# A graph-network kernel whose weight pieces are loaded in transfers of unequal height: 64, 24, 36 and 4 partitions in every third piece

## What is computed

```python
h = relu(layernorm(x))
q, k, v = h @ wq.T + bq, h @ wk.T + bk, h @ wv.T + bv
q2, k2, v2 = q @ wiq.T + biq, k @ wik.T + bik, v @ wiv.T + biv    # 16 heads of 64
scores = einsum('hnd,hmd->hnm', q2, k2) / 8 + mask                # mask: -inf where no edge
x = x + (softmax(scores) @ v2) @ wo.T + bo

h = relu(layernorm(x))
u = h @ root + bias
for r in range(8):                                                # mean over edges of type r
    u = u + (segment_sum(h[src] * (type == r), dst) / max(count, 1)) @ weight[r]
z = concat(u, h) @ w_gate + b_gate
x = x + tanh(u) * z + h * (1 - z)
```

## Time and profile before

| | us |
|---|---|
| median of three runs | 228.53 |
| the three runs | 226.64, 228.53, 229.94 |
| the profiled execution | 227.98 |
| its span | 225.8 |
| PE busy | 216.0 (96%) |
| DVE busy | 80.6 (36%) |
| POOL busy | 23.2 (10%) |
| ACT busy | 22.3 (10%) |
| packets of queue q1, share of 16 engines | 88.5% |

### The profile page before, as it was taken

The page is one execution under the profiler, slowest core; times in us unless marked ns, Lnnn a source line. Parts: engine busy times, 40 slices in busy tenths (PEclk is TensorE's granted clock), DMA queues, the critical chain, the costliest instruction groups (busy, mean ns, idle before and its releaser), DMA issues.

```text
span 225.8 us, 10194 instructions
## 1 busy us (share of the span) xinstructions
PE 216.0 (96%) x4797; PEld 210.1 (93%) x4797; DVE 80.6 (36%) x138; ACT 22.3 (10%) x41; POOL 23.2 (10%) x53
## 2 busy tenths in 40 slices
PE   2999998998999999999999999999999999999994
PEld 2889988998999999898999999999999999999993
DVE  2479638050399930555738500000000000000624
ACT  2550000000020110132033000000000000000101
POOL 2271005500000000010000940000000000000000
PEclk9999999999999999999999999999999999999999
DMA  6999999999999999999999799999999999998002
GB/s 225 366 393 422 421 422 421 380 376 385 363 386 385 328 383 376 363 359 399 412 360 379 209 306 398 328 383 388 398 380 361 369 350 338 356 363 332 6 3 70
DMA packets 14684, 77.01 MB, mean 341 GB/s; under 512 B 4874, under 2 KB 5138, under 8 KB 5428
## 3 DMA queue, kind: packets, MB, share of 16 engines
q1 hardware_dynamic: 14112, 75.96, 88.5%
q10 hardware_dynamic: 532, 0.42, 0.6%
HBM read 75.97 MB, written 0.39 MB: 338 GB/s over the span
## 4 chain that ended last, share of the span: by engine, by line
PE 95%; DMA 2%; issue 1%; DVE 1%; ACT 0%
PE acc L780 81%; PE acc L1027 4%; DMA x_sb<-in_x 2%; PE turn L968 1%; PE side L828 1%; PE side L968 1%; PE side L1027 1%; PE turn L856 1%; DVE stats L505 1%; PE acc L798 1%; PE turn L798 0%; PE turn L872 0%; PE side L839 0%; PE turn L839 0%; PE acc L872 0%
## 5 line engine op out<-in xcount | busy, mean ns | idle before, releaser
L780 PE MATMUL acc<-mean,raw 128*64 128x96 f32 x2048 | 84.7, 246 | 0.0
L780 PEld LDWEIGHTS acc<-mean,raw 128*64 128x64 f32 x2048 | 84.6, 137 | 0.0
L780 PE MATMUL acc<-hT,raw 128*64 128x96 f32 x1024 | 44.4, 247 | 0.3 <-issue 0.3
L780 PEld LDWEIGHTS acc<-hT,raw 128*64 128x64 f32 x1024 | 42.9, 137 | 1.4 <-issue 1.1
L743 DVE TENSOR_TENSOR uT<-acc,uT 128x384 f32<-128x384 f32 x2 | 1.1, 558 | 80.9 <-PE acc L780 80.9
L780 PE MATMUL acc<-kT,raw 128*64 128x96 f32 x512 | 22.1, 246 | 0.8 <-issue 0.8
L780 PEld LDWEIGHTS acc<-kT,raw 128*64 128x64 f32 x512 | 21.5, 137 | 1.3 <-issue 1.2
L780 PE MATMUL acc<-qT,raw 128*64 128x96 f32 x512 | 22.0, 246 | 0.7 <-issue 0.7
L780 PEld LDWEIGHTS acc<-qT,raw 128*64 128x64 f32 x512 | 21.4, 137 | 1.0 <-issue 1.0
L780 PE MATMUL acc<-uT,raw 128*64 128x96 f32 x256 | 12.6, 266 | 0.0
L780 PEld LDWEIGHTS acc<-uT,raw 128*64 128x64 f32 x256 | 12.2, 152 | 0.3 <-ACT uT L409 0.2
(11 more groups left out here) (177 smaller groups left out, 148.3 us busy)
## 6 DMA issues: line engine op xcount, KB each, us to landing
raw<-in_weights SPq DMA_DIRECT2D x284, 256.0 KB, 4.7
raw<-in_weights SPq DMA_DIRECT2D x1, 1024.0 KB, 5.9
x_sb<-in_x SPq DMA_DIRECT2D x1, 192.0 KB, 3.5
x_sb<-in_x ACTq DMA_DIRECT2D x1, 192.0 KB, 3.7
out<-out_rows SPq DMA_DIRECT2D x1, 192.0 KB, 2.1
out<-out_rows ACTq DMA_DIRECT2D x1, 144.0 KB, 2.4
out<-out_rows SPq DMA_DIRECT2D x1, 48.0 KB, 2.2
bias_rows<-in_biases ACTq DMA_DIRECT2D x1, 36.0 KB
```

Source lines behind the costliest of these rows:

```text
L780: mm = pe.matmul(a[g * HD:(g + 1) * HD, b, c * N:(c + 1) * N], raw[:, s, at:at + HD], moving(k0 + k), start=opens and k0 == 0 and c == 0 a ...
```

## The change

`transfers(n)` gets a second case. Every piece whose number leaves 1 when divided by 3 (1, 4, 7, ..., 70: 24 of the 72) is loaded in four transfers of unequal height: 64 partitions (all the even ones), 24 (the odd ones from 1 to 47), 36 (the odd ones from 49 to 119) and 4 (121, 123, 125, 127). Piece 0 and the other 47 pieces are loaded as they were. The bytes, the number of transfers and the semaphore counts stay.

```diff
 def transfers(n):
 
+
     if n == 0:
         return [slice(0, P)]
+    if n % 3 == 1:
+        return [slice(0, P, 2), slice(1, 49, 2), slice(49, 121, 2), slice(121, P, 2)]
     return [slice(j, P, 4) for j in range(4)]
```

## The result

The changed kernel took 272.23 us in the median of four runs (270.79 to 277.4), the kernel before 228.39 us beside it (226.64 to 229.94). The ratio is 1.190, with a 95% interval of 1.177 to 1.203: 19% slower. The forecast was 232.2 us and a range that ended at 240. The profiled execution of after has 270.79 us, its span 268.6 us against 225.8, 42.8 us more.

A forecast was written before the change was run, and what follows sets the result against it. PE, busy 216.0 of 225.8 us, was taken to bound the kernel. Weights staying hidden added nothing and late instructions 3.7 us (5.5 against 1.8), so 228.5 + 3.7 = 232.2 us, range 226.5 to 240.

The forecast's parts named there:

- its three gaps: PE's waits ending in "issue" at 29.7, 35.8 and 52.7 us, 1.8 us together, read as late instruction packets.
- How many engines share a transfer: Weight stream: largest divisor of the rows up to 16, so 64, 24, 36, 4 go to 16, 12, 12, 4 engines.
- A row costs 0.311 us whatever its transfer: Weight stream: engine time per 8 KB row, read from 30 to 34 us before the change and taken as fixed.
- Load of an engine in three pieces: DMA engines: 24 rows, 7.46 us before; after, 26 rows on four (8.09 us), 25 on eight, 20 on four.
- the first result: Weight stream: at 2.70 to 2.87 us a piece the last piece lands before 218.6 us, so weights stay hidden at no cost.
- the price of the second: PE's instruction fetch: packets late behind a lasting queue on the heavier engines, 5.5 us against 1.8, so +3.7 us.
- SP's issue of the short transfers: SP's issues of 24, 36 and 4 rows: 0.27 to 0.6 us each, so 7.6 to 8.6 us per three pieces.
- The bound from ACT's 274 ns: SP's issues: lower limit for short transfers, from one on 6 engines that ACT issued in 0.274 us.
- The rival with this end: Weight stream: narrow transfers at half rate, 3.11 us a piece against 2.97 allowed, weights late, 238 us; chance 0.10.
- Instructions late by 3.7 us more: PE's instruction fetch: the main case, late packets costing 5.5 us against 1.8, total 232.2 us; chance 0.44.
- The price of 0.36 us per late border: PE's instruction fetch: 1.8 us of gaps over 5 packet borders, charged per border while the queue is long.
- The upper bound of 18 us: Late-instruction term: long queue on all twelve engines to the end and gaps twice as long, +18 us.

The follow-up runs named there:

- f3: Kernel before with every third piece in two transfers of 64 partitions, even and odd, in place of four: 239.7 us, ratio 1.052.
- g4: Kernel before, with SP waiting ahead of the third transfer of each piece until the piece two before has landed: 233.7 us, ratio 1.020.
- k3: f3 with SP waiting in the middle of each piece until the piece two before has landed: 235.6 us, ratio 1.023.
- f2: Changed kernel with every third piece split 64, 16, 32, 16 instead, all on 16 engines with 8 rows each: 280.1 us, ratio 1.229.
- f4: Kernel before with every third piece in four equal transfers of 32 contiguous partitions: 333.9 us in two runs.
- k1: Kernel before with all pieces but the first in four transfers of 32 contiguous partitions: 346.2 us, ratio 1.516.
- k2: Kernel before with every third piece in step-4 transfers of 32, 32, 32, 24 and 8 rows: 248.8 us; 248.3 us when run again.
- m1: Changed kernel with the unequal transfers in every sixth piece in place of every third: 247.6 us, ratio 1.085.
- f1: Changed kernel with the transfers of 24 and 36 rows joined, so every third piece is 64, 60, 4: 284.1 us, ratio 1.247.
- g3: Kernel before, with SP waiting before each piece until the piece two before has landed: 258.1 us, ratio 1.133.
- k4: Kernel before, with SP's wait in mid-piece for the piece two before, for pieces 2 to 20 only: 230.6 us, ratio 1.010.

## Why the prediction was wrong, point by point

**PE is the bound and its three gaps are late instructions: right.** The gaps of after stand multiples of 256 instructions apart, each ends behind a packet of q8, f3 makes them grow with the queue while its rows stay fast, and g4 and k3 make them shrink.

**How many engines share a transfer: right.** q1 has 13632 packets, as worked out.

**A row costs 0.311 us whatever its transfer: wrong, and this is the step that failed.** "Load of an engine in three pieces" counted rows (26 against 24 on the heaviest engines) and priced them at the rate of the uniform stream. Equal loads (f2) gave the same slow rows as after. The row went from 0.347 to 0.428 us by the measure of the table, 23% on the whole stream, where the count of rows had given 8% on four engines. 72 x 8 x 0.428 = 247 us of stream, so it can't stay within the 2.97 us a piece that the lead allowed (3.42 now). With it fell the first result, that the weights stay hidden, and the price of the second, the late instructions, was far too low.

**SP's issue of the short transfers lies between 0.27 and 0.6 us: wrong.** L308 from 1.3 us on in after, two issues a line (min, median, max), so that each line hands one value to the next; the order is 128, 64, 24, 36 and 4 rows:

```profile
L308 SPq DMA_DIRECT2D raw<-in_weights x2: 408/481/554, 1.3 to 1.7; - x2
L308 SPq DMA_DIRECT2D raw<-in_weights x2: 554/702/850, 1.7 to 2.3; - x2
L308 SPq DMA_DIRECT2D raw<-in_weights x2: 743/796/850, 2.3 to 3.2; - x2
L308 SPq DMA_DIRECT2D raw<-in_weights x2: 611/677/743, 3.2 to 4.0; - x2
```

The transfer of 24 rows takes 850 ns, that of 36 743, that of 4 611, all above the 594 of 32 rows. Over the run the shortest of the 24 issues of each are 767, 743 and 611 ns. So these issues on 12 and 4 engines were longer than those on 16, not shorter. The bound from ACT's 274 ns was no bound. The first changed piece costs SP 554 + 850 + 743 + 611 = 2758 ns, where four of 32 rows cost 4 x 594 = 2376. All issues of weights together take 217.8 us in after and 188.7 before, 29 us more for the same number, and SP holds 19% of the chain. Not all of that is the form: in f4 and k1, from 60 to 200 us, issues of 32 rows take 1.07 and 1.00 us in the median.

**The weights stay hidden: wrong.** They follow from the two steps above: PE waits 10.7 us for raw. The rival with this end, transfers that collide in neighbouring partitions, had 0.10 and 238 us. It was the nearest in kind: rows slow down and the lead is used up. Its price was near too: 6 x 0.311 = 1.87 us for each engine and changed piece, where the table gives (0.428 - 0.347) x 9216 / 16 / 24 = 1.94. It came out low, 9.33 us for three pieces against 24 x 0.428 = 10.27, since it set all other rows at the best rate of 0.311 where their mean was 0.347 already, and it left out the late instructions. That the price fits is in part luck: it was counted as narrow rows alone, while k2 is slow with only 8 such rows, and in m1 and f4 the rows of other pieces slow down as well. Its argument against itself, that waiting engines work off other transfers meanwhile, did not hold.

**Instructions late by 3.7 us more: right in kind, more than five times too small.** It was 20.3 us more. The price of 0.36 us per late border came from a queue of 6 us, and was carried over to a run in which the queue is longer: a gap is now 22.1/15 = 1.5 us. The upper bound of 18 us, which I had built from all twelve engines and gaps twice as long and then put outside the range, was passed by 2 us. That bound rested on the load alone; in f1 and f2, with rows as slow and faster issues, the gaps are twice that.

**PE's busy time: not priced.** It grew by 11.5 us. The greater part is the granted clock. It is at the lower of its two levels (0.50, that is 1.2 GHz in place of 2.4) in four stretches of 3.4 us, from 23.7, 44.2, 78.3 and 208.0 us, each at the end of an idle stretch of PE of 2.2 to 2.7 us; one more idle stretch of 2.4 us, before 100.1, has no such fall. Before had 1.000 over the whole run. The windows view of after, one of these and one at the full clock:

```profile
78.30:81.70 3.40, 3.40 (x48) 3.40 (x46) 0.53 (x2) 0.00 (x0) 0.00 (x0) 0.50 1.04 340
50.00:53.40 3.40, 3.40 (x88) 3.40 (x86) 0.56 (x1) 0.00 (x0) 0.00 (x0) 1.00 1.04 246
```

48 matmuls where 88 pass at the full clock: some 1.6 us lost in each of the four, about 6 of the 11.5 us. The other 5 are not explained; waits too short to be taken as gaps are a guess.

**Open.** Which engine carries which rows, and so why engines that are out of step disturb each other in k2, was not seen: no view splits the packets by engine and partition. Every run with unequal numbers of rows also has transfers on fewer than 16 engines, so that the numbers and the match of engines to partitions can't be told apart. That they meet at a shared way into SBUF is an argument from k1, not shown for k2. Nor is it shown that instruction packets wait behind weights in the same queue; shown is that they come late when the queue is long, whatever made it long, and mostly on time when it is short.

## What to carry to other kernels

In a stream that keeps the DMA engines full, the form of every transfer counts. The safe form here was rows shared by all 16 engines and spread over the whole height, in every transfer. A third of the pieces cut otherwise cost 19%, and contiguous blocks of 32 cost 52%. And where an engine executes thousands of instructions, look at its gaps that end in "issue" and count the instructions between them: where the weights took long to land, the instructions were late too. A stream that is far ahead can so cost more than it gives. But pacing it with waits is no cure by itself: it took the gaps away and starved PE instead (g3 258.1, g4 233.7, k4 230.6 us against 228).

## What the runs showed of the hardware

- A row of 8 KB costs an engine about 0.32 us in a uniform stream and about 0.52 us while an unequal piece passes (m1); 0.6 us in a stream of contiguous blocks of 32 partitions (k1).
- Fewer, larger transfers made the kernel slower, 5% in f3, although they moved 420 GB/s. The Trainium skill (Runtime: NRT & Kernel Launch, instruction fetch mechanics) calls the crossing of a 16 KiB border "mostly hidden"; here it cost 0.6 us per late border with a queue of 5 to 7 us and 64.8 us in 29 gaps, 2.2 us each, with one of 32 us.
- The first issues on SP in after take 850, 743 and 611 ns for 24, 36 and 4 rows, and 554 for 64; the usual one of 32 rows takes 594.
- A gap of PE that ends in "issue" ends 1.2 to 1.8 us behind the landing of a 16 KB instruction packet, 194 times out of 194.
- PE's granted clock stood at 0.50 for 3.4 us behind four of five idle stretches of 2.2 to 2.7 us in after, 0.91 in the mean from 20 to 60 us, so that each of the four waits cost some 1.6 us on top of its own length.
